# A graph attention stage with the edge mask built by POOL and a new order on DVE and ACT

## The reference

```python
def _gat(h, adj, W, a, out_features):
    Wh = jnp.matmul(h, W)
    e = jnp.matmul(Wh, a[:out_features]) + jnp.swapaxes(jnp.matmul(Wh, a[out_features:]), 1, 2)
    scores = jnp.where(adj > 0, jax.nn.leaky_relu(e, negative_slope=0.2), -9000000000000000.0)
    return jnp.matmul(jax.nn.softmax(scores, axis=1), Wh)

h = _gat(_gat(x, adj, W1, a1, Fout), adj, W2, a2, W2.shape[1])
h = _layernorm(x + h, g_ln1, b_ln1)
ff = jnp.matmul(jax.nn.relu(jnp.matmul(h, w_ff1) + b_ff1), w_ff2) + b_ff2
x = _layernorm(h + ff, g_ln2, b_ln2)
```

## Time and profile before

| what | value |
|---|---|
| median of 3 runs | 1142.9 us (1141.55 to 1143.61) |
| profiled execution, its own time | 1141.11 us |
| its span, first to last instruction | 1139.3 us |
| granted TensorE clock, mean | 0.988 of full speed |
| busy: PE, DVE, ACT, POOL | 91%, 82%, 62%, 49% of the span |
| DVE, L834 (128 masks) | 87.3 us |
| ACT, L804 (128 exponentials) | 91.4 us |
| POOL, L1064 (16) and L453 (64) | 16.7 and 39.8 us |

### The profile page before, as it was taken

The page is one execution under the profiler, slowest core; times in us unless marked ns, Lnnn a source line. Parts: engine busy times, 40 slices in busy tenths (PEclk is TensorE's granted clock), DMA queues, the critical chain, the costliest instruction groups (busy, mean ns, idle before and its releaser), DMA issues. The chain is left out here.

```text
span 1139.3 us, 20494 instructions
## 1 busy us (share of the span) xinstructions
PE 1037.4 (91%) x5765; PEld 488.7 (43%) x5765; DVE 932.3 (82%) x2320; ACT 705.4 (62%) x1323; POOL 563.4 (49%) x506
## 2 busy tenths in 40 slices
PE   3588889888888799999999999999999999999997
PEld 3557667576664233333333333333333333244443
DVE  4898998989987778887888888888888888748787
ACT  2476777767765456665666666666666665654443
POOL 3112112121111388877887888888888887700000
PEclk9899999999999899999999999999999999999999
DMA  7131211312031313331433143223313330000001
GB/s 227 61 111 56 98 70 56 111 57 90 22 113 64 92 49 106 108 102 35 119 93 88 59 116 97 67 81 107 101 49 103 106 79 2 1 10 29 37 28 46
DMA packets 49279, 86.85 MB, mean 76 GB/s; under 512 B 8376, under 2 KB 35256, under 8 KB 44219
## 3 DMA queue, kind: packets, MB, share of 16 engines
q1 hardware_dynamic: 47018, 85.59, 24.6%
q10 hardware_dynamic: 2192, 0.47, 0.2%
HBM read 52.19 MB, written 29.36 MB: 72 GB/s over the span
## 5 line engine op out<-in xcount | busy, mean ns | idle before, releaser
L1597 DVE TENSOR_REDUCE top<-b_peak 128x1 f32<-128x512 f32 x488 | 320.3, 684 | 73.9 <-PE b_peak L1273 72.6
L1438 ACT ACTIVATE b_prob<-b_score 128x1024 f32<-128x1024 f32 x256 | 258.1, 1025 | 151.9 <-PE b_score L1288 106.2
L1787 POOL TENSOR_TENSOR b_picked<-b_prob,mask 128x512 f32<-128x512 f32 x192 | 234.2, 1240 | 58.1 <-ACT b_prob L1438 45.8
L1787 POOL TENSOR_TENSOR b_picked<-b_prob,b_mask 128x512 f32<-128x512 f32 x185 | 226.1, 1243 | 56.6 <-ACT b_prob L1438 46.1
L1064 POOL TENSOR_TENSOR a_hw_n<-a_hw,a_inv 128x512 f32<-128x512 f32 x16 | 16.7, 1043 | 221.7 <-issue 168.4
L804 ACT ACTIVATE a_att<-a_att,a_least 128x512 f32<-128x512 f32 x128 | 91.4, 715 | 32.4 <-DVE a_least L834 32.4
L1273 PE MATMUL b_peak<-b_k_stack,b_q_stack 96*128 96x512 bf16 x256 | 98.4, 384 | 6.6 <-DVE top L1597 6.2
L1273 PE MATMUL b_peak<-shared 96*128 96x512 bf16 x232 | 90.0, 389 | 7.5 <-DVE top L1597 4.0
L834 DVE CUSTOM_DVE_ANT_0 a_att<-a_att,a_no_edge 128x512 f32<-128x512 f32 x128 | 87.3, 700 | 0.0
L550 PE MATMUL a_mid<-a_h_t,wff 128*128 128x512 f32 x128 | 64.9, 626 | 14.4 <-ACT a_hid L798 12.8
L1288 PE MATMUL b_score<-shared 98*128 98x512 bf16 x256 | 77.3, 383 | 0.0
(11 more groups left out here) (230 smaller groups left out, 1891.9 us busy)
## 6 DMA issues: line engine op xcount, KB each, us to landing
a_adj_in<-in_adj SPq DMA_DIRECT2D x15, 1024.0 KB, 5.1
scratch<-shared SPq DMA_DIRECT2D x32, 384.0 KB, 3.0
shared<-scratch SPq DMA_DIRECT2D x16, 768.0 KB, 6.9
scratch<-shared SPq DMA_DIRECT2D x32, 256.0 KB, 2.1
b_q_stack<-scratch SPq DMA_DIRECT2D x8, 768.0 KB, 5.5
b_k_stack<-scratch SPq DMA_DIRECT2D x8, 768.0 KB, 8.2
a_x_t<-in_x_t SPq DMA_DIRECT2D x16, 256.0 KB, 2.6
xs<-in_x SPq DMA_DIRECT2D x16, 256.0 KB, 5.3
```

Source lines behind the costliest of these rows:

```text
L1438: act.activation(prob[s % 2][:, 2 * u:2 * u + 2, :], score[u][:, :, :], ACT.Exp, scale=float(DH) ** -0.5).then_inc(sem("exp_ready"), 1)
L1597: dve.tensor_reduce(top[g][:, hh, c:c + 1], peak[hh % 2][:, :], AX.X, ALU.max, negate=True).then_inc(sem("peak_read"), 1)
L1787: pool.tensor_tensor(picked[(NR * s + rel) % 2][:, hh, :], prob[s % 2][:, hh, :], m, ALU.mult).then_inc(sem("picked_pool"), 1)
```

## The change

The work done is the same. The mask of edges moves from DVE to POOL, as two instructions over 128x2048 with a semaphore of its own between them: clamp the codes to 0 or 1, then times -`MASKED` plus `MASKED`. In POOL's step it stands behind `scale_hw` and ahead of `encode`. On DVE, `scores(0, ..)` calls the inversion of the other round behind its first mask, not its second, and `add_h` behind its second, not ahead of its third; `scale_rows` follows at once and does its own inversion in two pieces, three chunks and one; `norm_shift` moves ahead of `add_x`, and `keep_hw` ahead of `first_shift`. On ACT, `keep_x` moves from the end of a step to behind the next step's `keep_h`, and the four `hidden` come each ahead of its exponentials.

```diff
@@ scalar engine, step @@
                 if feed:
                     keep_h(t - 3)
+                    if t >= 4:
+                        keep_x(t - 4)
...
-                for chunks, chunk in (((0,), 0), ((), 1), ((1,), 2), ((2, 3), 3)):
+                for chunk, chunks in enumerate(((0,), (1,), (2, 3), ())):
+                    if feed:
+                        hidden(t - 3, chunk)
                     if second:
                         exps(1, t - 2, chunks)
-                    if feed:
-                        hidden(t - 3, chunk)
...
-                if feed:
-                    keep_x(t - 3)
@@ vector engine @@
                 for c in chunks:
                     if c + 1 < C:
                         leak(k, b, c + 1, s2)
-                    if c == 2:
+                    mask(k, b, par, c)
+                    if c == 0:
+                        invert_other()
+                    if c == 1:
                         add()
-                    mask(k, b, par, c)
-                    if c == 1:
-                        invert_other()
...
             def scale_rows(b):
                 dve.wait_ge(hw_done, b)
-                dve.wait_ge(inv_ready[0], b + 1)
-                for c in range(C):
-                    last = dve.tensor_scalar(xw_n[:, c, :], xw[:, b, c, 0:D + 2], inv[0][:, c:c + 1], None, ALU.mult)
+                for n, chunks in enumerate((range(C - 1), range(C - 1, C))):
+                    at = slice(chunks[0], chunks[-1] + 1)
+                    dve.wait_ge(exp_ready[0], C * b + chunks[-1] + 1)
+                    dve.reciprocal(inv[0][:, at], total[0][:, at]).then_inc(inv_ready[0], 1)
+                    dve.wait_ge(inv_ready[0], 2 * b + n + 1)
+                    for c in chunks:
+                        last = dve.tensor_scalar(xw_n[:, c, :], xw[:, b, c, 0:D + 2], inv[0][:, c:c + 1], None, ALU.mult)
                 last.then_inc(scaled[0], 1)
...
+                if first:
+                    scale_rows(t - 1)
                 if feed:
                     norm_stats(1, t - 3)
-                if first:
-                    invert(0, t - 1)
-                    scale_rows(t - 1)
+                    norm_mean(1, t - 3)
...
                 if feed:
-                    norm_mean(1, t - 3)
+                    norm_shift(t - 3)
                 if second:
                     add_x(t - 2)
-                if feed:
-                    norm_shift(t - 3)
-                if second:
                     norm_stats(0, t - 2)
                     norm_mean(0, t - 2)
-                if begin and t != 1:
-                    edges(t, par)
+                if first:
+                    keep_hw(t - 1)
                 if second:
                     first_shift(t - 2)
-                if first:
-                    keep_hw(t - 1)
-                if begin and t == 1:
-                    edges(t, par)
-                if second:
                     finish_rest(t - 2)
                 if begin:
+                    dve.wait_ge(code_ready, C * t + C)
                     see(t)
@@ gpsimd @@
                 if second:
                     scale_hw(t - 2)
+                if begin:
+                    edges(t, par)
                 if more:
                     if first:
                         pool.wait_ge(scaled[0], t)
                     encode(pool, t + 1, range(C))
...
+            def edges(b, par):
+
+                if not (isinstance(b, int) and b < 2):
+                    pool.wait_ge(masked[1], C * (b - 1))
+                pool.wait_ge(code_ready, C * b + C)
+                pool.tensor_scalar(no_edge[par][:, :, :], codes[:, b, :, :], 1.0, 0.0, ALU.min, ALU.max).then_inc(edge_found, 1)
+                pool.wait_ge(edge_found, b + 1)
+                pool.tensor_scalar(no_edge[par][:, :, :], no_edge[par][:, :, :], -MASKED, MASKED, ALU.mult, ALU.add).then_inc(edge_ready, 1)
```

More of the change, by code:

```diff
@@ L402, in graph_layer @@
         row_ready = [sem(f"row_ready{k}") for k in range(2)]
-        edge_ready = sem("edge_ready")
+        edge_ready, edge_found = sem("edge_ready"), sem("edge_found")
         low_ready = [sem(f"low_ready{k}") for k in range(2)]
@@ L671, in step @@
                     lower(1, t - 2)
+                elif first:
+                    lower(0, t - 1)
                 if feed:
                     keep_h(t - 3)
+                    if t >= 4:
+                        keep_x(t - 4)
                 if begin:
@@ L680, in step @@
                     act.copy(xw[:, t, :, :].rearrange("p (a c) d -> p a (c d)", a=2), both).then_inc(xw_ready, 1)
-                if first:
+                if second:
                     lower(0, t - 1)
-                for chunks, chunk in (((0,), 0), ((), 1), ((1,), 2), ((2, 3), 3)):
+                for chunk, chunks in enumerate(((0,), (1,), (2, 3), ())):
+                    if feed:
+                        hidden(t - 3, chunk)
                     if second:
                         exps(1, t - 2, chunks)
-                    if feed:
-                        hidden(t - 3, chunk)
                 if first:
@@ L707, in tail @@
                 keep_h(B - 3)
+                keep_x(B - 4)
                 act.wait_ge(scaled[0], B - 1)
@@ L800, in exps @@
             def exps(k, b, chunks):
-                act.wait_ge(inv_ready[k], b)
+                act.wait_ge(inv_ready[k], (2 - k) * b)
                 for c in chunks:
@@ L979, in tail @@
                 add_h(B - 3)
-                invert(0, B - 1)
                 scale_rows(B - 1)
@@ L1021, in tail @@
                 most(22, 24)
[L1023 to L1027, removed]
             def add_h(b):
```

## The result

The changed kernel takes 1166.42 us (median, 1164.53 to 1166.7) against 1142.88: the ratio is 1.0206, with a 95% interval of 1.0193 to 1.0219. It is slower by 1.9 to 2.2%, clear of the noise, and 2.6 us under the forecast of 1169. The profiled execution took 1166.57 us, its span is 1164.8, the mean granted clock 0.988 as before.

A forecast was written before the change was run, and what follows sets the result against it. DVE, the fullest engine, and what holds it up were taken to set the first stage's step. Thirteen steps add 24.4 us, the first two 2: 1141.1 + 26.4 = 1167.5 profiled, so 1169 median; range 1147 to 1187.

The forecast's parts named there:

- Holding: First stage: a POOL instruction reading SBUF holds a DVE instruction with two SBUF inputs for its whole length; step 1.88 us longer.
- The path given back sooner, or a fourth mask ahead of the second POOL instruction: Rival at the fourth mask: step 20.53 us, time 1145, or near 1167 if the scaling is held; chance 0.15.
- the faster case: Rival: long POOL instructions do not hold the masks; step 19.63 to 20.36 us, time 1133 to 1143; chance 0.08.
- E: Length of each new POOL instruction over 128x2048: 1.91 us, with 1.5 as lower end and 2.46 as upper.
- inversion for `scale_hw`: DVE in `scores(0, ..)`: comes right behind the first mask, at 7.02 us into the step.
- M: Moment the fourth mask of `scores(0, ..)` leaves DVE: 13.54 us into the step, where it was 11.00 before.
- from M to the next leak: Rest of the step behind the fourth mask: 8.71 us, where it was 9.37 before.
- The `keep_x` that I called hidden by ACT's idle time: On ACT: 0.66 us, gone from ahead of `lower` to behind `keep_h`, where it was to cost nothing.
- All gains together: Behind the fourth mask: L1027, `keep_x` and the split inversion, against exposed waits for ACT, gain 0.66 us a step.
- The first steps: First two steps: they collide too but have idle time of their own; 2 us added for both, an estimate.
- `edges(0)`: POOL's edges at the start: hidden by the wait for the second adjacency, so no cost.
- The tail: After the thirteen steps: keeps its order but for the split inversion and one moved `keep_x`; change of nothing.

The follow-up runs named there:

- Behind the masks: The changed kernel with POOL's wait for the scaled rows ahead of its two edge instructions, so they run after the masks: 1164.15 us, ratio 1.0196.
- the last experiment: The kernel after with edges made by ACT, `turn_y` in the middle of round two, and several other orders changed: 1127.97 us, ratio 0.9874.
- the run without the reads: The changed kernel with both new POOL instructions replaced by memsets of the same tile, which read no SBUF: 1141.99 us, measured once.
- the order alone: The kernel after with its new DVE and ACT order, but the edges made by one DVE instruction as before: 1149.57 us, ratio 1.0071.
- the move alone: The kernel before with its old order, but the edges made by two POOL instructions ahead of encoding: 1189.74 us, ratio 1.0419.

## Why the prediction was right, and where its terms were off

**The mechanism.** Holding is shown from four sides: by its mark in the trace (0.48 us from POOL's end to DVE's next), by memsets that do not hold the masks, by pieces that hold for a piece, and by one instruction that holds one mask. The path given back sooner, or a fourth mask ahead of the second POOL instruction, did not happen: that mask took 2.36 us. Nor did the faster case; E was 1.9, above the 0.97 from which it would have decided.

**The length E.** Forecast 1.91 from the slope of two short instructions. Behind the masks, where no mask disturbs them, the two take 1.89 us (L1061, 245.89) and 1.90 (L1063, 247.87). The 2.33 and 2.22 in the kernel after are these with a wait for a mask in them.

**The walk through the step**, in us from its first leak:

| event | forecast | measured |
|---|---|---|
| inversion for `scale_hw` | 7.02 | 7.40 |
| `scale_hw` ends | 8.40 | 8.79 |
| second mask leaves | 8.88 | 9.27 |
| third mask leaves | 11.21 | 11.57 |
| fourth mask leaves (M) | 13.54 | 13.86 |
| from M to the next leak | 8.71 | 8.47 |
| step | 22.25 | 22.33 |

Two small errors, which nearly cancel; that the step comes within 0.1 us is luck to that extent. I let the inversion follow the mask at once; but ACT's last exponential of the other round now ends 7.30 into the step (241.44), where it ended 6.87 into it before, and DVE waits 0.30 us. The `keep_x` that I called hidden by ACT's idle time stands ahead of these exponentials:

```profile
235.09 0.77 ACT L781 ACTIVATE xs<-a_mid,columns 128x512 f32<-128x512 f32 x1
```

The new place of `hidden` does not explain the wait: in the last experiment `hidden` has its old place and `keep_x` the new one, and that exponential ends 7.42 into the step, with DVE waiting 0.42 us. No run moves `keep_x` alone. And the part behind M is 0.24 shorter than I put together, since `norm_stats` starts at M + 1.36, not 1.6.

**The gains of the order.** "All gains together ... 0.66 us a step" sized only what lies behind M; it measured 9.37 - 8.47 = 0.90. Ahead of M the new order loses as much: with memsets in POOL's place M is 11.91 (251.51 - 239.60), not 11.00, by the wait for ACT and by the mask beside `scale_hw`. And from M to the next leak it is then 8.75, a gain of 0.62 only: the scaling waits 0.35 us for ACT's exponential, which in the kernel after is done while the masks are held. Without any holding by the new instructions the step is 20.66, which is 0.29 longer than before, although L1027 is gone. In the sum this loss was hidden inside the held masks. Of the 25.6 us that thirteen steps lost, (20.66 - 20.37) x 13 = 3.8 are the order's and (22.34 - 20.66) x 13 = 21.8 are the new instructions'. The rival that I called faster, 1133 to 1143 with 1138 in the middle, was put too low with it: the run without the reads gives 1142, in part because its step 3 begins 1.9 us sooner (53.64) than before.

**The sum.** Thirteen steps: 25.6 against 24.4. The first steps: I added 2; step 3 starts at 55.35 against 55.49, so they cost nothing. That is two errors that cancel. With the order alone step 3 starts at 49.30, a gain of 6.2 us that I had put at nothing, and POOL's edges take 6.05 of it back, three times the 2 that I counted. In step 1 the masks and the scaling are held (3.70 us for three scalings of 0.68), but that step's leaks begin 3.3 us sooner (4.3 with the order alone, at 12.25). Before, ACT ended their wait; now POOL's `edges(0)` does, which I had called hidden. The kernel after, then the kernel before:

```profile
13.24 1.41 DVE L830 SCALAR_TENSOR_TENSOR a_att<-a_row,a_s_own,a_low 128x512 f32<-128x512 f32 x2 [3.92 <-POOL a_no_edge L1063]
...
19.66 3.70 DVE L909 TENSOR_SCALAR a_xw_n<-shared,a_inv 128x130 f32<-128x130 f32 x3
...
16.57 1.41 DVE L827 SCALAR_TENSOR_TENSOR a_att<-a_row,a_s_own,a_low 128x512 f32<-128x512 f32 x2 [5.98 <-ACT a_low L785]
```

The edit behind it is a line of the change that I did not price: in that one step `lower(0, ..)` stands ahead of the copies that `begin` makes on ACT. The timelines of ACT bear it out: `lower` starts at 11.56, with the copies at 15.17 behind it, where it started at 15.82 behind the copies at 15.27. No run has this line alone. The tail takes 1164.8 - 345.82 = 818.98 us against 1139.3 - 320.37 = 818.93: nothing, as forecast. Together 25.5 us of span, against 26.4.

## What to carry to other kernels

Ahead of moving work to POOL, list DVE's instructions that read two tensors of SBUF, or scale from SBUF to SBUF, and lay POOL's new instructions over them: each that meets one waits for what is left of it, however small it is itself, and POOL goes between two masks that stand back to back. POOL's free time is no measure. Long POOL instructions belong beside leaks, reductions and instructions fed from PSUM, or in pieces, or the work goes to ACT. And taking time from the busiest queue brings little before the loop through all engines has been added up from start to start; here it ran over DVE, PE and ACT. Letting half of a ready matmul group go ahead of one that waits for a late input, with some smaller changes of order, took 0.76 us from the step (20.26 to 19.50), where the instruction that had been moved was worth 0.1.

## What the hardware showed that I had not expected

- The scaling of rows (L909, a `tensor_scalar` from SBUF to SBUF) is held as well: 3.70 us for three in step 1, and 1.14 us beside short POOL pieces, against 0.68 free. For it a memset is enough, which does not hold the masks (1.73 us for one piece, against 0.29). No row of the kernel before had shown it.
- An idle PE costs twice. With the move alone PE idles 2.44 us ahead of round one, and in eight of thirteen steps the granted clock then falls to the lower level for a part of it (0.51 from 241 to 243 us), round one taking 5.26 us instead of 3.82. The five others idle as long and stay at 1.00, and why is open. With 0.98 us of idle, in the kernel after, the windows show 1.00.
- POOL's time did not depend on the size of the input's elements in these runs: 128x2048 takes 1.89 us from int8 to bfloat16 and 1.90 from bfloat16 to bfloat16, 0.92 ns an element all told. A memset of the same tile takes 1.80 or 1.81.
